# The four b1 products of a mixture-of-experts kernel issued as one group in four row tiles

## The reference

```python
h = layernorm(x) * (1 + ca) + sa            # sa, ca, ga, sb, cb, gb: six rows per batch, from c
x = x + ga * ssm(h)                         # silu(h @ Win + bin), a decaying scan, @ Wout + bout
h = layernorm(x) * (1 + cb) + sb
p = softmax(h @ Wr + br)                    # 8 experts; each token goes to its best 2
# each expert e, for its tokens (D = 128, F = 512):
a = layernorm(relu(h @ W1[e] + b1[e])) * g1[e] + be1[e]
y = layernorm(relu(a @ W2[e] + b2[e])) * g2[e] + be2[e]
x = x + gb * (the two experts' y of each token, weighted by its two normalised probabilities)
```

## Time and profile before

| | |
|---|---|
| median of 3 runs (lowest to highest) | 515.25 us (514.6 to 516.82) |
| span of the profiled execution (first to last instruction) | 512.1 us |
| busy share of the span: PE, PEld, DVE, ACT, POOL | 95%, 75%, 86%, 82%, 71% |
| granted TensorE clock, mean over the span | 0.985 of 2.4 GHz |
| start of tile 8's and of tile 132's L1561 | 182.11 us, 478.09 us |

### The profile page before, as it was taken

How to read it: one execution, slowest core, us unless ns; L and a number is a source line. 1 busy time by engine, 2 the same in 40 slices (tenths; PEclk the granted TensorE clock), 3 DMA queues, 4 the chain that set the end, 5 groups by cost and what they waited for, 6 DMA issues and landing times. The chain is left out here.

```text
span 512.1 us, 14684 instructions
## 1 busy us (share of the span) xinstructions
PE 486.5 (95%) x3051; PEld 386.3 (75%) x3051; DVE 440.3 (86%) x2217; ACT 420.4 (82%) x1148; POOL 364.3 (71%) x483
## 2 busy tenths in 40 slices
PE   7989999999985899999999999999999999999994
PEld 6446656555544798998989799998999989999951
DVE  7779899998887698888888799988989999898894
ACT  6678887978764688888888798899989889999883
POOL 1004665666667778888888888888888888888871
PEclk9999999999997899999999999999999999999998
DMA  6980111145111789677515785677677677567555
GB/s 166 312 240 27 44 47 48 47 131 111 55 44 52 166 154 172 188 191 198 163 64 158 187 221 152 184 205 176 164 207 191 162 189 206 151 187 214 164 173 164
DMA packets 79786, 77.78 MB, mean 152 GB/s; under 512 B 11150, under 2 KB 72745, under 8 KB 79702
## 3 DMA queue, kind: packets, MB, share of 16 engines
q1 hardware_dynamic: 71286, 59.92, 47.2%
q0 software_dynamic: 8416, 16.93, 9.2%
HBM read 54.65 MB, written 22.59 MB: 151 GB/s over the span
## 5 line engine op out<-in xcount | busy, mean ns | idle before, releaser
L646 POOL DMA_INDIRECT expert_rows<-rows_ring,slot x128 | 123.3, 963 | 93.6 <-issue 76.3
L674 POOL DMA_INDIRECT expert_results<-y,target x119 | 123.0, 1034 | 30.7 <-issue 26.2
L1672 PE MATMUL bank<-W,h2T 128*128 x720 | 95.4, 275 | 0.8 <-ACT h2T L773 0.3
L1672 PEld LDWEIGHTS bank<-W,h2T 128*128 128x128 f32 x720 | 87.7, 192 | 9.1 <-issue 1.4
L870 ACT ACTIVATE v<-wmod 128x128 f32<-128x128 f32 x135 | 42.0, 311 | 39.1 <-DVE vg L1373 35.5
L1362 DVE SCALAR_TENSOR_TENSOR wmod<-bank,rse,shifts 128x128 f32<-128x128 f32 x119 | 41.6, 350 | 30.8 <-PE bank L1672 25.9
L1561 PE MATMUL bank<-b_parts,onesr 128*128 x135 | 64.9, 481 | 1.2 <-DVE h3lo L1140 1.2
L758 ACT ACTIVATE n<-X,nm,rs 128x128 f32<-128x128 f32 x128 | 54.1, 486 | 8.0 <-DVE nm L1307 8.0
L1145 DVE BATCH_NORM_STATS2 stf<-h1T 128x6 f32<-128x512 f32 x90 | 59.2, 658 | 0.0
L1569 PE MATMUL bank<-ident_wr,h1T 128*128 128x128 f32 x360 | 54.5, 274 | 0.0
L1562 PE MATMUL bank<-W1hi,h3hi 128*128 x135 | 53.8, 399 | 0.0
(11 more groups left out here) (250 smaller groups left out, 1229.0 us busy)
## 6 DMA issues: line engine op xcount, KB each, us to landing
shifts<-expert_shifts SPq DMA_DIRECT2D x119, 192.0 KB
hrow<-expert_rows SPq DMA_DIRECT2D x135, 65.0 KB
xi<-expert_results SPq DMA_DIRECT2D x12, 512.0 KB, 5.3
out_x<-X SPq DMA_DIRECT2D x15, 256.0 KB
X<-in_L_attn_x SPq DMA_DIRECT2D x7, 512.0 KB, 7.4
W1lo<-in_L_ffn_W SPq DMA_DIRECT2D x4, 512.0 KB, 6.7
expert_rows<-rows_ring,slot POOLq DMA_INDIRECT x128
expert_results<-y,target POOLq DMA_INDIRECT x119
```

The lines of the kernel that those rows point to most:

```text
L646: nc.gpsimd.indirect_dma_start(out=rows_d, out_offset=bass.IndirectOffsetOnAxis(ap=slot[q][:, n // TOPK, n % TOPK:n % TOPK + 1], axis=0), ...
L674: nc.gpsimd.indirect_dma_start(out=results_d, out_offset=bass.IndirectOffsetOnAxis(ap=target[i % TARGETS][:], axis=0), in_=y[k], in_offset ...
L1672: ins = mm(acc, rT[(s - 4) % DEPTH][:, ch * P:(ch + 1) * P], W2[:, bass.ds(e4 * CF + ch, 1), :], start=(ch == 0), stop=(ch == CF - 1))
```

## The change

`b1_parts` and its zeros go. b1's two parts are stored in HBM (`b1_d`, for each expert two rows of 512), and each tile's two rows are loaded into a ring `b1_ring` with two turns: the four tiles 4k to 4k+3 have their rows at partitions 0 and 1, 32 and 33, 64 and 65, 96 and 97 of one turn. SP issues these loads (`load_b1`) for four tiles at once, eight tiles ahead, in front of the load of rows of the first of them.

TensorE issues the four b1 products of tiles 4k to 4k+3 together at the start of `hidden(4k)` (`biases`), each with two partitions, into four banks: the first product now goes round the banks 1, 2, 3 and 0. Each tile's three W1 products then add to its bank in its own step. For the two banks that this takes, the turned result is now always in bank 4 and the second product always in bank 5. So three waits change: `biases(i)` waits until all first products up to tile i-1 are evicted; `turn_hidden(i)` waits until the turned result of tile i-1 is evicted; the second product of tile s-4 waits until VectorE has read the values of tile s-5 (before: s-6).

ScalarE's order in a step, high part and then first product, is the same in both kernels. Two semaphores of the setup are merged into others.

```diff
+        b1_ring = sb("b1_ring", [P, 2, F], F32R)
+        def b1_rows(i):
+            first = i % TOGETHER * QUARTER
+            return slice(first, first + 2), i // TOGETHER % 2
+        hidden_banks = [bank[n] for n in (1, 2, 3, 0)]
+        turned_bank, value_bank = bank[4], bank[5]
...
+            def load_b1(i):
+                load_expert_numbers(i)
+                if i >= 2 * TOGETHER:
+                    sp.wait_ge(h_done, i - 2 * TOGETHER + 1)
+                for n in together(i):
+                    part, turn = b1_rows(n)
+                    sp.dma_start(b1_ring[part, turn, :].bitcast(F32), b1_d[bass.ds(expert_of[n], 1), :, :].rearrange("o k f -> (o k) f")
+                                 ).then_inc(b1_loaded[turn], 16)
...
                 if i % AT_ONCE == 0:
                     load_row_numbers(i)
+                    load_b1(i)
...
-            for e in range(E):
-                ins = nc.scalar.activation(b1_parts[:, e, :], padding[:, TAGS:TAGS + 1].broadcast_to([P, F]), ACT.Copy)
...
+            def biases(i):
+                pe.wait_ge(b1_loaded[i // TOGETHER % 2], b1_count(i))
+                pe.wait_ge(r_ready, i)
+                for n in together(i):
+                    part, turn = b1_rows(n)
+                    mm(hidden_bank(n)[:], onesr[part, :], b1_ring[part, turn, :], start=True, stop=False)
             def hidden(i):
+                if i == 0:
+                    pe.wait_ge(h3lo_ready, EARLY_H)
+                if i % TOGETHER == 0:
+                    biases(i)
                 pe.wait_ge(h3lo_ready, i + 1)
-                if i >= 2:
-                    pe.wait_ge(r_ready, i - 1)
-                mm(h, onesr[:], b1_parts[:, bass.ds(e, 1), :], start=True, stop=False)
...
             def turn_hidden(i):
                 pe.wait_ge(r_ready, i + 1)
+                pe.wait_ge(rT_ready, i)
...
-                    if on(s - 6, EXPERT_TILES):
-                        pe.wait_ge(v0_ready, s - 5)
+                    if on(s - 5, EXPERT_TILES):
+                        pe.wait_ge(v0_ready, s - 4)
```

More of the change, by code:

```diff
@@ L65, in adaln_ssm_moe_kernel @@
     gates_d = nc.dram_tensor("gate_b_rows", (1, B * D), F32, kind="Internal").ap()
+    b1_d = nc.dram_tensor("b1_two_parts", (E, 2, F), F32, kind="Internal").ap()
     with ExitStack() as ctx:
@@ L118, in adaln_ssm_moe_kernel @@
         b1hi = third_rT[0:E, :]
-        b1_parts = sb("b1_parts", [P, E, F], F32R)
+        TOGETHER = 4
+        QUARTER = P // TOGETHER
+        b1_ring = sb("b1_ring", [P, 2, F], F32R)
         onesr = sb("onesr", [P, P], F32R)
@@ L282, in last_user, with together, b1_count, hidden_bank @@
             return max((m for m in range(i) if ring(m) == ring(i)), default=None)
+        def together(i):
+            return range(i, min(i + TOGETHER, EXPERT_TILES))
+        def b1_rows(i):
+            first = i % TOGETHER * QUARTER
+            return slice(first, first + 2), i // TOGETHER % 2
+        def b1_count(i):
+            return 16 * sum(len(together(n)) for n in range(i % (2 * TOGETHER), i + 1, 2 * TOGETHER))
+        hidden_banks = [bank[n] for n in (1, 2, 3, 0)]
+        def hidden_bank(i):
+            return hidden_banks[i % len(hidden_banks)]
+        turned_bank, value_bank = bank[4], bank[5]
         early01 = [t[:].rearrange("p c l -> p (c l)").rearrange("p (j k) -> p j k", j=J) for t in xi]
@@ L316, in adaln_ssm_moe_kernel @@
         gb_stored, gb_loaded, b1_stored = sem("gb_stored"), sem("gb_loaded"), sem("b1_stored")
+        b1_loaded = [sem(f"b1_loaded{n}") for n in range(2)]
         (n1_ready, t1_done, h1T_ready, xi0_done, xi1_done, xi0_ready, xi1_ready, z_done,
@@ L478, in _ @@
             AT_ONCE = 4
+            assert TOGETHER == AT_ONCE
             row_of, expert_of = {}, {}
@@ L526, in _ @@
                 load_rows(n, n)
+            for n in range(0, SLOTS, TOGETHER):
+                load_b1(n)
             for n in range(SLOTS - SHIFT_LAG):
@@ L768, in hidden @@
                 act.wait_ge(h_done, i + 1)
-                nc.scalar.activation(r[i % DEPTH], bank[1 + i % 2][:], ACT.Relu).then_inc(r_ready, 1)
+                nc.scalar.activation(r[i % DEPTH], hidden_bank(i)[:], ACT.Relu).then_inc(r_ready, 1)
             def hidden_turned(i):
                 act.wait_ge(tr_done, i + 1)
-                nc.scalar.activation(rT[i % DEPTH], bank[3 * (1 - i % 2)][:], ACT.Copy).then_inc(rT_ready, 1)
+                nc.scalar.activation(rT[i % DEPTH], turned_bank[:], ACT.Copy).then_inc(rT_ready, 1)
             def mixer_step(s, q, e, k):
@@ L1361, in values @@
                 dve.wait_ge(rse_ready, s - 4)
-                vec.scalar_tensor_tensor(wide(v0[p]), wide(bank[4 + p][:, 0:D]), rse[q][:, 0:1],
+                vec.scalar_tensor_tensor(wide(v0[p]), wide(value_bank[:, 0:D]), rse[q][:, 0:1],
                                          wide(shift_rows[k5][:, 0:D]), ALU.mult, ALU.add).then_inc(v0_ready, 1)
@@ L1553, in turn_rows @@
                 tr(to, hrow[row_slot][:, H], ident[:]).then_inc(t3_done, 1)
-            def hidden(i):
-                e, q = expert_of[i], i % 2
-                h = bank[1 + q][:].rearrange("p (o f) -> p o f", o=1)
+            def biases(i):
[4 more added lines that the diff above has]
+                    mm(hidden_bank(n)[:], onesr[part, :], b1_ring[part, turn, :], start=True, stop=False)
+            def hidden(i):
+                e = expert_of[i]
+                h = hidden_bank(i)[:].rearrange("p (o f) -> p o f", o=1)
+                if i == 0:
+                    pe.wait_ge(h3lo_ready, EARLY_H)
+                if i % TOGETHER == 0:
+                    biases(i)
                 pe.wait_ge(h3lo_ready, i + 1)
-                if i >= 2:
-                    pe.wait_ge(r_ready, i - 1)
-                mm(h, onesr[:], b1_parts[:, bass.ds(e, 1), :], start=True, stop=False)
                 mm(h, h3hi[i % DEPTH], W1hi[:, bass.ds(e, 1), :], start=False, stop=False)
@@ L1567, in turn_hidden @@
                 pe.wait_ge(r_ready, i + 1)
+                pe.wait_ge(rT_ready, i)
                 for ch in range(CF):
-                    ins = tr(bank[3 * (1 - i % 2)][:, ch * P:(ch + 1) * P], r[i % DEPTH][:, ch * P:(ch + 1) * P], ident[:])
+                    ins = tr(turned_bank[:, ch * P:(ch + 1) * P], r[i % DEPTH][:, ch * P:(ch + 1) * P], ident[:])
                 ins.then_inc(tr_done, 1)
@@ L1663, in expert_step @@
                     e4 = expert_of[s - 4]
-                    acc = bank[4 + q][:, 0:D].rearrange("p (o d) -> p o d", o=1)
+                    acc = value_bank[:, 0:D].rearrange("p (o d) -> p o d", o=1)
                     pe.wait_ge(rT_ready, s - 3)
-                    if on(s - 6, EXPERT_TILES):
-                        pe.wait_ge(v0_ready, s - 5)
+                    if on(s - 5, EXPERT_TILES):
+                        pe.wait_ge(v0_ready, s - 4)
                     if s == TABLE2_STEPS:
```

32 lines of the change are left out of this document (12 added, 20 removed).

## The result

The changed kernel takes 530.5 us (median of four runs, 529.8 to 531.0) against 515.4 of the kernel before beside it: a ratio of 1.029, 95% interval 1.027 to 1.032, 15 us slower. The profiled execution has a span of 528.5 us; before it was 512.1, so 16.4 us are to be found.

The account below looks back on a forecast made before the run. TensorE, never waiting in a 2.37 us step, was taken as the bound. -30.1 + 21.8 + 21.5 - 0.4 - 0.2 = +12.6 on 512.1 gives 524.7, plus 3.15 makes 528 us; range 511 to 543 (own case 520 to 537).

Parts of the forecast that it names:

- The b1 product leaves each step: TensorE, every expert step: dropping the full b1 product saves 0.23, 131 times, -30.1 us; a step without a group takes 2.14.
- The group, 0.66: TensorE, every fourth tile: four weight loads in a row, then one product, cost 0.66 a group, 33 times, +21.8 us.
- The rival "entirely together": Rival on TensorE's four b1 products: they run as one, a group costs 0.23, 514 us, no change; chance 0.15.
- The estimate of 0.30 a group: Beside the 0.66 a group on TensorE: by the skill page's measured row-tile speedup, 0.30 a group and 516 us.
- The wait, 0.58 and 0.92: TensorE at group starts waits for ScalarE's eviction: 26 times 0.58, seven times 0.92 with pieces of the sum, +21.5 us.
- The rival "no wait": Rival at group starts: the eviction chain falls below 2.22, TensorE finds the bank free, 21.5 less, 506 us; chance 0.10.
- The single banks: Turned result and second product with one bank each: waits put at nothing, up to 0.1 in steps with a piece.
- that sign of being wrong: TensorE's waits for the turned result's bank showing up in short steps would make the forecast wrong; no size given.
- SP and the late rows: SP's four more load issues per group, 2.2 us, mostly hidden; TensorE's waits for late rows shrink: -0.4, bounds -0.9 and +4.4.
- The start, "at nothing": First group, ahead of the later 33: lies where TensorE waits for others anyway, put at nothing.
- the setup's 0.2: Setup: eight zero copies that hold ScalarE until 7.59 go, while its input stood at 7.31; less the signal, -0.2 us.
- whose steadiness it asked for in the late stretches alone: Sign of being wrong: TensorE's granted clock falling below 1.00 in the profiled late stretches of the expert stage.

Follow-up runs that it names:

- the group twice: The changed kernel with all four b1 products of each group issued two times in a row, the second writing the same: 535.5 us, 1.040.
- the kernel that moved the second product: The changed kernel, but in each fourth step the four b1 products and the tile's W1 products come behind the second product: 521.6 us, 1.013.
- ScalarE's order: The changed kernel, but in steps that start a group ScalarE evicts the first product ahead of the next tile's high part: 522.8 us, 1.013.
- the moved group: The changed kernel, but in each fourth step the tile's three W1 products come first and the four b1 products behind them: 513.7 us, 0.996.
- the kernel with the idle products: The changed kernel with 16 extra TensorE products ahead of the first hidden products, where it waits for VectorE: 530.1 us, 1.026.

## Why the prediction held, step by step

The mechanism of the expert stage held, and the time came out 2.5 us over the forecast. In spans the miss is larger, 16.4 against 12.6: the 3.15 that the prediction adds from span to median is 2.0 in the kernel after, and this luck hides a part of it. Between tiles 8 and 132 lie 93 short steps, 24 ordinary group steps and 7 in groups 84 to 108.

*The b1 product leaves each step: right.* Short steps are 2.13 to 2.19 but for 14 of 93, mean 2.172. Tile 14's (2.57) holds two extra products of the table, as a step of 2.80 does before; tile 15's is 2.67, tile 86's 2.51, and eleven are 2.21 to 2.27, nine of them between tiles 90 and 110.

*The group, 0.66: right in size, for another reason.* I had four weight loads of 0.11 in a row and then a product. In the trace the four loads lie within 0.22 and the products within 0.51; the runs with groups of one, two and four tiles and no wait give 0.62, 0.61 and 0.59, and the doubled group adds 0.23. So a group is one product's 0.23 and up to 0.39 that goes with any number of narrow products: 0.18 ahead of them and 0.21 behind, where the next full product starts 0.44 after the first narrow one, and its weight load, with 0.25 of idle time before it, only then. The Trainium skill, "TensorEngine Tiling (Array Packing)", "Key Properties", says that different tiles can load weights and multiply in parallel; I had read past that sentence, and these rows agree with it. Its other sentence, that a change of mode drains TensorE, fits both, though no run here separates a drain from any other cost of the change. The rival "entirely together" had the four products right and failed on the price of the change to narrow products and back: it gave 0.23 for a group. The estimate of 0.30 a group, from the 3.07 times of the Trainium skill, "TensorE: Matmul & The Clock Gate", "Measured speedup vs the span model", falls with it.

*The wait, 0.58 and 0.92: right, a little larger in groups with pieces.* Ordinary group steps are 3.29 on average, 2.14 + 0.62 + 0.53; in groups 84 to 108 they are 3.80, so the wait there is 1.04. Both are what is left of the step beside 2.14 and 0.62; around tile 32 it is seen directly, as the group starts 1.08 behind the transposes where 0.53 is usual without a wait. For the 31 groups that is 24 x 0.53 + 7 x 1.04 = 20.0 us, by the forecast's terms 20.4. It was reasoned that the chain runs at VectorE's and ScalarE's pace and does not shrink with TensorE's work; the wait put alone into the kernel before cost the same, and what helped was to come later or to move ScalarE's eviction forward. The rival "no wait" fell with that: what a stop gave was used up in three steps.

*The single banks: right but for a little.* In the kernel after one wait of 0.2 shows for the turned bank, at tile 86, so that sign of being wrong did come, once. Only the kernel that moved the second product found the value bank late in every group; those with ScalarE's order or the moved group wait two to four times for VectorE's values, 0.9 to 1.3 us in all. *SP and the late rows: a little more gained.* The two long steps before (3.02 and 3.34 at tiles 51 and 54) are gone, 1.6 us, where 0.4 was taken.

Together, for tiles 8 to 132: -124 x 0.23 + 31 x 0.62 + 20.0 - 1.6 = +9.1, and the short steps' 0.03 over 2.14 (93 x 0.032 = 3.0, less what the steps of before have over 2.37, the late rows left out, 0.5) make it 11.6; measured 11.7, and 11.9 by the forecast's terms for that stretch. As the waits are remainders, the 11.6 checks the counting and not the waits; these rest on the runs above.

*The start, "at nothing": the step that failed.* Of the 5.0 us ahead of tile 8 the forecast had 1.1 (two groups less five b1 products, less the setup's 0.2): it put the first group at nothing and had no term for the clock there, whose steadiness it asked for in the late stretches alone. In the kernel after TensorE's clock is at half, 1.2 GHz, from 153.5 to 167 and again from 170.6 to 180.8; before, it is back at full after 159 and, the second time, after 172.8. The W1 products of tiles 1, 4 and 8 come 1.4, 2.1 and 5.0 us later than before (0.5 of it stands already ahead of the experts' first tile, where the setup's gain of 0.2 does not show: traces with one and the same setup differ there by up to 1.4); the steps that end with tiles 4, 5 and 6 take 3.53, 4.07 and 2.89. With the group twice and the clock at full the last two take 2.16 and 2.14, so half the clock costs 2.66 in these two steps alone.

Why the second stretch lasts 10 us here stays open. TensorE was not idle in it: from 171.6 to 180.8 it was busy but for 0.1. In the profiled executions of the kernel with the idle products it lasts 10 us too, with the group twice, the moved group or ScalarE's order 3.4. But the moved group together with ScalarE's order, the same instructions as the moved group up to tile 3, stands at half from 154.6 to 175.1 without a break, and four executions of the group twice have mean clocks of 0.981 and 0.980 (533.6 and 534.7 us) and 0.974 and 0.976 (536.3 and 537.2). So it is not the kernel's alone, and one trace does not tell kernels apart here. All four executions of the kernel after lie at 0.974 to 0.976, all of the kernel before at 0.982 to 0.988. Filling the idle stretch at 153.5 did not bring tile 8 forward in the execution that was profiled.

## What to carry to other kernels

Narrow products in row tiles among full ones cost up to 0.39 us a time here beside their own 0.23, however many stand together. By these figures a group breaks even at three full products of 0.23 that it replaces; with four it saves 0.3, if nothing waits. Before putting work of several tiles together, look at what all their buffers must have come free of: the group waits for the latest, and a place 0.7 us later in the same step took that wait away. When TensorE gets faster, read on which engine has the least room at which tiles: here GpSimd kept some 3 to 5 of 24 us. And read the granted clock ahead of the steady stage too: here it cost 2.66 us in two steps.

## What the runs showed of the hardware

Four b1 products of two rows each, in four row tiles and four banks, take the time of one (0.23 more for four more), and even their weight loads lie within 0.22 us. One narrow product alone costs 0.62 between full ones, against 0.23 for the full product with 126 rows of zeros.
A stop of TensorE costs more than the wait shown for it: behind an eviction that ended at 243.98 the next product starts 0.24 later, and in the kernel after, behind one that ended at 246.17, the group starts 0.14 later.
The clock can stay at half under a busy TensorE: from 171.6 to 180.8 us it was granted 0.50, busy but for 0.1 us; with the group twice nearly the same instructions ran at 1.00 from 173.2 on.
